# Linear attention and a 3x3 convolution on 32 images: set-up rewritten, value and output weights joined per head, order changed, last image written out

## The reference

```python
# layer 0: linear attention, 4 heads of 32 channels, 4 learned memory positions
xn  = x / norm * g * C ** 0.5                    # norm over channels, of the group-normed x
q, k, v = split(einsum('bchw,oc->bohw', xn, w_qkv))
k, v = concat([mem_k, k]), concat([mem_v, v])    # along the pixels
q = softmax(q, over the head's channels) * dh ** -0.5
k = softmax(k, over pixels)
context = einsum('bhdn,bhen->bhde', k, v)
out = einsum('bhde,bhdn->bhen', context, q)
x = x + einsum('bchw,oc->bohw', out, w_out) + b_out
# layer 1: 3x3 convolution where (j - i) % 4 == 0, 1x1 convolution elsewhere
x = x + conv3x3(gn(x), w3 * m3) + einsum(w1 * ~m3, gn(x)) + b1.sum(axis=1)
```

## Time and profile before

| what | value |
|---|---|
| median of 3 runs | 2020.36 us (2018.03 to 2023.75) |
| the profiled execution, its time | 2011.88 us |
| its span, first to last instruction | 2010.1 us |
| mean granted TensorE clock | 0.983 of full |
| busy: PE, DVE, ACT, POOL | 94%, 83%, 68%, 66% |
| DMA queue of the loads, stores and copies | 73.8% of 16 engines |

### The profile page before, as it was taken

One profiled execution on the slowest core, in us unless ns is written; L12 is line 12 of the kernel. 1 busy time (PEld: TensorE's weight loads), 2 busy tenths in 40 slices (PEclk: granted clock), 3 DMA queues, 4 the chain that ended last, 5 costly groups with the idle time before them and its releaser, 6 DMA issues.

```text
span 2010.1 us, 50737 instructions
## 1 busy us (share of the span) xinstructions
PE 1882.8 (94%) x21199; PEld 1017.6 (51%) x21199; DVE 1676.3 (83%) x3144; ACT 1361.0 (68%) x1476; POOL 1321.8 (66%) x737
## 2 busy tenths in 40 slices
PE   2889999999999999999999999999999999999995
PEld 0445545555544555554555554455554455555452
DVE  5688888888888888888888888888888888888862
ACT  2667668767667776766876766777766777676660
POOL 5566667776667676666776665777666767666652
PEclk9789999999999999999999999999999999999997
DMA  5358778787877797876878777778787778787665
GB/s 108 64 96 176 162 159 162 160 177 160 165 162 160 156 183 154 174 163 159 161 161 170 165 163 156 154 167 177 152 175 154 162 155 180 148 174 162 130 132 129
DMA packets 349427, 312.96 MB, mean 156 GB/s; under 512 B 299152, under 2 KB 299920, under 8 KB 341008
## 3 DMA queue, kind: packets, MB, share of 16 engines
q1 hardware_dynamic: 347712, 308.73, 73.8%
q10 hardware_dynamic: 1168, 0.98, 0.2%
q0 software_dynamic: 320, 0.01, 0.0%
HBM read 68.10 MB, written 67.11 MB: 67 GB/s over the span
## 4 chain that ended last, share of the span: by engine, by line
PE 66%; DVE 17%; SPq 9%; DMA 4%; issue 2%; ACT 1%; POOL 0%; ACTq 0%
PE pair_ps L813 21%; PE pair_ps L795 8%; PE pair_ps L756 6%; PE pair_ps L804 4%; PE bank_ps L710 4%; DVE u L1121 4%; DVE km L1124 3%; PE pair_ps L776 3%; SPq L320 2%; DVE yg_lo L1171 2%; SPq L333 2%; DVE image L1176 2%; DVE bn L1045 2%; PE bank_ps L786 2%; PE pair_ps L741 2%; PE bank_ps L765 2%
## 5 line engine op out<-in xcount | busy, mean ns | idle before, releaser
L813 PE MATMUL pair_ps<-replicas,w_rep 96*32 96x512 f16 x8192 | 490.5, 384 | 11.7 <-DMA replicas<-yg_lo 11.3
L441 POOL TENSOR_TENSOR u_lo<-u,u_hi 128x1024 f16<-128x1024 f32 x128 | 270.3, 2144 | 274.3 <-ACT u_hi L558 274.3
L444 POOL TENSOR_TENSOR exp_kT_lo<-exp_kT,exp_kT_hi 128x1024 f16<-128x1024 f32 x128 | 273.6, 2137 | 206.4 <-ACT exp_kT_hi L567 203.4
L813 PEld LDWEIGHTS pair_ps<-replicas,w_rep 96*32 96x32 f16 x8192 | 204.4, 96 | 260.1 <-issue 85.2
L447 POOL TENSOR_TENSOR u_lo<-exp_q,u_hi 128x1024 f16<-128x1024 f32 x128 | 272.6, 2141 | 45.5 <-ACT u_hi L573 44.7
L558 ACT ACTIVATE u_hi<-u 128x1024 f16<-128x1024 f32 x128 | 134.9, 1054 | 134.8 <-DVE u L1121 130.1
L1176 DVE SCALAR_TENSOR_TENSOR image<-pair_ps,image 128x512 f32<-128x512 f32 x256 | 176.0, 688 | 55.0 <-PE pair_ps L813 49.4
L437 POOL TENSOR_SCALAR u<-image,st 128x1024 f32<-128x1024 f32 x128 | 179.6, 1411 | 40.4 <-DVE st L1075 40.4
L564 ACT ACTIVATE exp_kT<-pair_ps,zcol 128x1024 f32<-128x1024 f32 x128 | 142.0, 1109 | 90.3 <-PE pair_ps L756 87.7
L573 ACT ACTIVATE u_hi<-exp_q 128x1024 f16<-128x1024 f32 x128 | 133.9, 1046 | 97.1 <-DVE exp_q L1163 97.1
L454 POOL TENSOR_TENSOR yg_lo<-u,yg_hi 128x1024 f16<-128x1024 f32 x64 | 152.9, 2390 | 68.5 <-ACT yg_hi L581 68.5
(11 more groups left out here) (179 smaller groups left out, 4601.2 us busy)
## 6 DMA issues: line engine op xcount, KB each, us to landing
image<-in_x SPq DMA_DIRECT2D x256, 256.0 KB, 4.8
out<-image SPq DMA_DIRECT2D x512, 128.0 KB, 2.3
replicas<-yg_hi SPq DMA_DIRECT2D x256, 165.0 KB, 3.6
replicas<-yg_hi SPq DMA_DIRECT2D x256, 107.2 KB, 2.3
replicas<-yg_lo SPq DMA_DIRECT2D x128, 165.0 KB, 4.1
replicas<-yg_lo SPq DMA_DIRECT2D x128, 107.2 KB, 2.3
uT_hi<-u_hi SPq DMA_TRANSPOSE x128, 4.4
uT_lo<-u_lo SPq DMA_TRANSPOSE x128, 4.2
```

The source lines that it names most:

```text
L441: pool.tensor_tensor(px(UL, v), px(U, v), px(UH, v), ALU.subtract).then_inc(ul_ready, 1)
L444: pool.tensor_tensor(KL[:, v % 2], KT[:, v % 2], KH[:, v % 2], ALU.subtract).then_inc(kl_ready, 1)
L813: mm = pe.matmul(conv_ps[32 * r:32 * r + 32, j % 2], w_rep[0:32 * SLOTS, tap, r], rep[:, j * ROWS + dy:(j + 1) * ROWS + dy, dx:dx + SIDE], ...
```

## The change

Four things change together.

**Set-up.** SP waits until image 0 has landed before it issues the loads of image 1. ACT permutes the weights (three copies), DVE no longer does, and so `x_seed` and `x_scale` of image 0 don't stand behind them. PE turns query, key and output weights first and ten convolution blocks after them; the value weights aren't turned. ACT keeps the turned taps in SBUF after the first `norm_power`, rounds them after the last `high_u` of image 0, and DVE splits them behind the first `rows_q`; SP replicates the convolution weights after step 1 instead of step 0. Four large memsets go to DVE (`spread` and `minus_max` were POOL's).

**Per head.** The set-up multiplies value weights and output weights of each head into `value_out` (128 x 4 x 128) and the memory values into `memory_out`. `value_context` and `mask_context` are gone; `mix_weights` has eight float32 products of 128x32 weights on 128 columns, each head on its own column group. Context and memory part are turned undivided, and `split_mix` divides.

**Order.** `square_y` 2 and 3 follow `exp_memory`, `y_moments` follows `max_q` 2, `x_stats` 0 stands before `rows_q` and `low_y` 0 before the other three, `queries` 3 uses another pair, `norm_sums` stand elsewhere, and more, as the diff has it.

**The end.** `over_samples` makes 33 steps instead of 35, and then `drain(c, e)` writes out the end of image 31 (c) and of 30 (e): DVE makes its group norm and low parts alone, the replicating DMAs and stores are shared by SP and ACT, and the statistics of image 31 start before the last chunks of image 30.

SP, before the loop, in `step` and in `drain`:

```diff
-for k in range(PRELOADED):
-    load(k, 0)
-    load(k, 1)
+load(0, 0)
+load(0, 1)
+for h in range(2):
+    sp.wait_ge(x_in[h][0], at_load(0))
+load(1, 0)
+load(1, 1)
...
+        if e is not None:
+            sp.wait_ge(out_ready, at(e, CHUNKS, 6))
+            store(e, 2)
         if a is not None:
             sp.wait_ge(ul_ready, at(a, UNITS, 1))
             turn_u(a, 0)
...
+def drain(c, e):
+    sp.wait_ge(hi_ready, at(c, UNITS, 2))
+    sp.wait_ge(conv_done, at(e, CHUNKS, 4))
+    replicate_high_part(c, 0, range(2))
+    sp.wait_ge(lo_even, at(c, UNITS // 2, 1))
+    sp.wait_ge(lo_odd, at(c, UNITS // 2, 1))
+    replicate_low_part(c, 0, range(2))
...
+    sp.wait_ge(out_ready, at(c, CHUNKS, 8))
+    store_part(c, 3, range(2))
```

ACT, in `norm_power`, `high_u`, `step` and `drain`, and before the loop:

```diff
+        if first(s):
+            act.wait_ge(setup_pe, TAPS_TURNED)
+            act.activation(taps32[:, 0:8], conv_ps.rearrange("p k (t o) -> p (k t) o", o=P), ACT.Copy,
+                           scale=W_SCALE).then_inc(setup_act, 1)
...
+        if first(s) and v == UNITS - 1:
+            act.wait_ge(setup_act, TAPS_KEPT)
+            act.activation(w_hi, taps32[:, 0:TAPS], ACT.Copy).then_inc(setup_act, 1)
...
             exp_memory()
+        if c is not None:
+            act.wait_ge(y_ready, at(c, UNITS, 3))
+            square_y(c, 2)
+            act.wait_ge(y_ready, at(c, UNITS, 4))
+            square_y(c, 3)
+        if a is not None:
             act.wait_ge(kT_done, at(a, UNITS, 1))
...
+            act.wait_ge(q_soft, at(a, UNITS, 3))
+            high_q(a, 2)
         if p is not None:
             act.wait_ge(norm_sum, at(p, UNITS, 2))
             act.wait_ge(xg_ready, at(p, UNITS, 4))
             square(p, 3)
...
+def drain(c, e):
+    act.wait_ge(y_ready, at(c, UNITS, 3))
+    square_y(c, 2)
+    act.wait_ge(y_ready, at(c, UNITS, 4))
+    square_y(c, 3)
+    act.wait_ge(y_stat, at(c, Y_STEPS, Y_STEPS))
+    high_y(c, 0)
+    high_y(c, 1)
...
+    replicate_high_part(c, 0, range(2, RES))
+    high_y(c, 2)
+    act.wait_ge(conv_done, at(e, CHUNKS, 8))
+    high_y(c, 3)
...
+    replicate_low_part(c, 0, range(2, RES))
...
+act.wait_ge(weights_in, 16 * WEIGHT_DMAS)
+act.activation(perm_qkv, raw_qkv.rearrange("p t (i r) -> p t r i", r=RES), ACT.Copy).then_inc(setup_act, 1)
+act.activation(perm_w1, raw_w1.rearrange("p (i r) -> p r i", r=RES), ACT.Copy).then_inc(setup_act, 1)
+act.activation(perm_w3, raw_w3.rearrange("p (i r t) -> p t r i", r=RES, t=TAPS), ACT.Copy).then_inc(setup_act, 1)
```

PE, its functions, `step` and `drain`:

```diff
+def fold_values():
+    pe.wait_ge(setup_dve, HEADS_READY)
+    heads = wo_heads.rearrange("p h o -> p (h o)")
+    pe.matmul(pair_ps[0][:, 0:BANK], perm_qkv[:, 2].rearrange("p r i -> p (r i)"), heads, start=True, stop=True)
+    pe.wait_ge(col_in, 16 * COL_DMAS)
+    pe.matmul(pair_ps[0][0:MEM, BANK:2 * BANK], mv[:], heads, start=True, stop=True).then_inc(setup_pe, 1)
...
     def norm_sums(s, v, ps):
...
+        if first(s) and v == UNITS - 1:
+            fold_values()
...
-    def value_context(ps):
-        pe.matmul(ps[:, 0:P], wqkvT[:, 2], AT_sb[:], start=True, stop=False)
-        pe.matmul(ps[:, 0:P], mvT[0:MEM], pkT_sb[0:MEM], start=False, stop=True).then_inc(mix_pe, 1)
     def mix_weights(ps):
-        pe.matmul(ps[:, 0:P], ctxT_sb[:], woT[:], start=True, stop=True).then_inc(mix_pe, 1)
+        for h in range(HEADS):
+            q = slice(DH * h, DH * h + DH)
+            pe.matmul(ps[q, 0:P], AT_sb[:, q], value_out[:, h], start=True, stop=False)
+        for h in range(HEADS):
+            q = slice(DH * h, DH * h + DH)
+            mm = pe.matmul(ps[q, 0:P], pkT_sb[:, q], memory_out[:, h], start=False, stop=True)
+        mm.then_inc(mix_pe, 1)
...
             pe.wait_ge(k_max, at(a, 8, 7))
             turn_k_max(bank_ps[1])
+            rough_q(a, 0, pair_ps[1])
...
         if c is not None:
             conv_dense(c, 0)
+        if a is not None:
+            pe.wait_ge(den_act, at(a, 2, 1))
+            pe.wait_ge(mix_dve, at(a, 7, 2))
+            turn_context(bank_ps[1])
+        if c is not None:
             conv_dense(c, 1)
...
             conv_ring(c, 0)
             conv_ring(c, 1)
         if a is not None:
             pe.wait_ge(den_dve, at(a, 4, 4))
             den_broadcast(a, 0, pair_ps[1])
         if p is not None:
+            if a is not None:
+                pe.wait_ge(mix_dve, at(a, 7, 5))
             pe.wait_ge(sq_ready, at(p, UNITS, 1))
             norm_sums(p, 0, bank_ps[1])
             pe.wait_ge(sq_ready, at(p, UNITS, 2))
             norm_sums(p, 1, bank_ps[1])
         if a is not None:
+            den_broadcast(a, 1, pair_ps[0])
+        if c is not None:
+            pe.wait_ge(out_ready, at(c, CHUNKS, 1))
+            conv_dense(c, 2)
+        if a is not None:
+            pe.wait_ge(q_soft, at(a, UNITS, 1))
+            den_broadcast(a, 2, pair_ps[1])
+        if c is not None:
+            conv_ring(c, 2)
+        if a is not None:
+            mix_weights(bank_ps[0])
+            pe.wait_ge(q_soft, at(a, UNITS, 3))
             den_broadcast(a, 3, pair_ps[1])
+        if c is not None:
+            pe.wait_ge(out_ready, at(c, CHUNKS, 2))
+            conv_dense(c, 3)
+        if a is not None:
+            pe.wait_ge(mix_dve, at(a, 7, 7))
+            pe.wait_ge(el_ready, at(a, UNITS, 1))
+            mix(a, 0, pair_ps[0])
         if p is not None:
             pe.wait_ge(sq_ready, at(p, UNITS, 3))
             norm_sums(p, 2, bank_ps[1])
             pe.wait_ge(sq_ready, at(p, UNITS, 4))
             norm_sums(p, 3, bank_ps[1])
...
+def drain(c, e):
+    pe.wait_ge(out_ready, at(e, CHUNKS, 5))
+    conv_dense(e, 6)
+    pe.wait_ge(y_stat, at(c, Y_STEPS, 4))
+    group_means(1, bank_ps[1], y_group)
+    conv_ring(e, 5)
+    conv_ring(e, 6)
...
+    conv_ring(e, 7)
+    pe.wait_ge(out_ready, at(e, CHUNKS, 7))
+    pe.wait_ge(lo_even, at(c, UNITS // 2, 1))
+    conv_dense(c, 0)
```

DVE, its functions, `step` and `drain`:

```diff
     def norm_guard(s, ps):
...
+        if first(s):
+            dve.wait_ge(setup_pe, FOLDED)
+            dve.tensor_scalar(value_out[:].rearrange("p h o -> p (h o)"), pair_ps[0][:, 0:BANK], gcol[:], None, ALU.mult)
+            make(dve.tensor_copy(memory_out[0:MEM].rearrange("p h o -> p (h o)"), pair_ps[0][0:MEM, BANK:2 * BANK]))
...
+                dve.tensor_scalar(kneg_bf[:, 32:33], km[:, 5:6], -1.0, None, ALU.mult)
+                did(dve.tensor_scalar(kneg_bf[:, 0:1], km[:, 5:6], -1.0, None, ALU.mult))
...
+                did(dve.tensor_tensor(z[:, 0:1], ps[:, P:P + 1], pk_sum[:], ALU.add), wait=False)
+                did(dve.tensor_copy(A_sb[:], ps[:, 0:P]))
+                did(dve.reciprocal(z[:, 1:2], z[:, 0:1]), wait=False)
...
             max_q(a, 1, pair_ps[0])
+            dve.wait_ge(q_rough, at(a, UNITS, 3))
+            max_q(a, 2, pair_ps[1])
         if c is not None:
             dve.wait_ge(y_squared, at(c, UNITS, 4))
             y_moments(c)
...
             x_stats(p, 0)
+        if a is not None:
+            dve.wait_ge(max_turned, at(a, 2, 2))
+            rows_q(a, bank_ps[1])
+        if c is not None:
+            dve.wait_ge(yg_ready, at(c, UNITS, 1))
+            dve.wait_ge(hi_ready, at(c, UNITS, 1))
+            low_y(c, 0)
+        if p is not None and not first(p):
             x_stats(p, 1)
...
+def drain(c, e):
+    dve.wait_ge(y_squared, at(c, UNITS, 4))
+    y_moments(c)
...
+    finish(e, 5)
+    group_norm_y(c, 0)
...
+    last_low_y(c, 2)
+    dve.wait_ge(conv_done, at(e, CHUNKS, 7))
+    finish(e, 6)
+    dve.wait_ge(conv_done, at(e, CHUNKS, 8))
+    finish(e, 7)
```

More of the change, by code:

```diff
@@ L676, in step @@
                     square_y(a, 1)
-                    act.wait_ge(y_ready, at(a, UNITS, 3))
-                    square_y(a, 2)
-                if p is not None:
-                    act.wait_ge(u_ready, at(p, UNITS, 1))
-                    high_u(p, 0)
-            act.wait_ge(setup_pe, 1)
-            for t in range(0, TAPS, 4):
-                n = min(4, TAPS - t)
-                last = act.activation(w_hi[:, t:t + n], tap_ps(t, n).rearrange("p (t o) -> p t o", t=n), ACT.Copy,
-                                      scale=W_SCALE)
@@ L772, in queries @@
             def queries(s, v, ps):
+                if first(s) and v == 0:
+                    pe.wait_ge(const_made, POOL_STEPS)
                 for j in (2 * v, 2 * v + 1):
@@ L1311, in _ @@
+            for t in (kneg_bf, quad_mask, red_norm, red_head):
                 last = dve.memset(t[:], 0.0)
```

439 lines of the change are left out of this document (257 added, 182 removed).

## The result

The changed kernel takes 1961.03 us (median of 4 executions, 1959.35 to 1965.83) where the kernel before took 2022.05 us on the same chip: ratio 0.9704, 95% interval 0.9688 to 0.9721. The forecast was 1962 us, in the range of 1942 to 1987 us. On a second chip the same pair gave 1963.47 and 2013.96 us, ratio 0.9752 (0.9727 to 0.9777). The profiled execution took 1962.26 us, its span is 1960.5 us; the span before was 2010.1 us, so 49.6 us have to be found in the trace.

The account below looks back on a forecast made before the run. PE was taken to bound the steady state, 85% of the span. Gains of 37 us in the steps, 10 at the start and 11 at the end make 58: 2020.4 - 58 = 1962 us, range 1942 to 1987.

Parts of the forecast that it names:

- Small products: PE's eight new value and output weight products take 0.65 us instead of 1.15: gain 0.5 us a step.
- Norm sums: PE's second pair of `norm_sums` no longer waits for ACT's last square: gain 0.6 us a step, bounds 0 and 0.6.
- PE's 1.1 us arrive as about 0.8: Behind a step's first ring products, PE's 1.1 us gain shrinks to about 0.8 because DVE's residual and norm chain limits it.
- Context wait: PE's wait for the context's DVE steps shrinks from 0.34 to 0.1 us a step.
- Group mean of layer 1: `y_moments` behind `max_q` 2 makes PE wait a new 0.3 us before this mean, in front of keys 2.
- Statistics: PE's wait for the next image's statistics mostly goes with DVE's new order: 0.55 of 0.60 us a step gained.
- Ring 0's wait: At a step's first ring products, more steps wait for `low_y` replicas issued by SP: 0.1 us a step lost.
- Sum a step: Steady state: 1.2 us a step gained, 58.4 instead of 59.64, times 31 is 37 us; bounds 0.4 to 1.7.
- Start: First norm broadcast at 37.5 us instead of 47.64: gain 10 us, bounds 6 and 12.
- End: Last image: shorter waits for low parts and replicas, last store and low-clock time: gain 11 us, bounds 7 and 14.
- first rival: Steady gain only a third, through poorly overlapping column groups, late squares or DVE's chain: 1987 us, chance 16%.
- third rival: More gain than forecast, since unprofiled runs have more long steps that go too: 1949 to 1954 us, chance 9%.

Follow-up runs that it names:

- second of before: The kernel before, unchanged, executed and profiled once more: ratio 1.0007 to before, span 2016.4 us against 2010.1 in its first trace.
- image 1 at once: The changed kernel with SP loading image 1 right behind image 0, without waiting for image 0 to land: ratio 0.9768 to the kernel before.

## Why the prediction was right

The total was right, 61 us (50 on the second chip) for 58. That it came within 1 us of the forecast is in part luck: between the two profiles there are 49.6 us, the steps brought less than forecast and the ends more, and the replicas' wait, 12 us in 31 steps more than forecast, was made up for by the long steps that the first profile had too few of (11.4 us between the medians and the profiles). The sum a step also left out what the prediction itself had found ahead of ring 0, 0.3 and 0.15 us of new waits against 0.25 us gained; the 0.2 us did not come. The parts, step by step:

- **Small products**: 0.55 us for 0.65, gain 0.60 for 0.5, the upper bound. The argument that column groups run beside each other holds.
- **Norm sums**: both pairs together take 1.99 us instead of 2.77 (1.10 and 1.67), gain 0.78 for 0.6. As a mechanism right; but its price with the place taken away, 1.8 us in the shortest step, was underestimated by far, because I stopped at ACT's square and did not follow the residuals behind it.
- **"PE's 1.1 us arrive as about 0.8"**: the reason was wrong. Behind ring 0 the shortest step lost 0.56 us (24.18 to 23.62), and no new wait for DVE is there. The rest went into the broadcasts of the denominators: before, two of them stood together, four products in 0.32 us (a row at 1039.31 below); now each stands alone, two products in the same 0.32 us (1253.89 to 1254.21, 1255.21 to 1255.53, 1258.92 to 1259.24). That costs 0.64 us a step, and the prediction did not price it. 0.60 + 0.78 - 0.64 is 0.74; the 0.18 left is in products of the mix and dense products that are parted now.
  On PE's timeline of the kernel before, two broadcasts and the dense product behind them:

```profile
1039.31 0.40 PE L717 MATMUL pair_ps<-parts,spread 32*128 32x512 bf16 x4
1039.63 0.62 PE L804 MATMUL pair_ps<-yg_hi,w_mid 128*128 128x512 f16 x2
```

- **Context wait** 0.34 to 0.1: it is gone. **Group mean of layer 1**, 0.3 us of new wait: it did not come. **Turned key maxima** +0.15: 0.23. Together the shortest step is 0.19 us shorter ahead of ring 0.
- **Statistics**: the wait is gone, as forecast, 0.54 us a step in this trace and 0.74 in the second of before. That DVE's new order removes it is shown for the kernel before. In the new order of the other engines it isn't `low_y` 0's place: back in the old one only 0.2 us a step of the wait return.
- **Ring 0's wait**: the term that was mis-sized. I named SP's list and took 0.1 us a step for it; the wait grew by 0.49 us a step. The sentence before it, that nothing ahead of ring 0 can be gained beyond the short step since SP's list is the same, was nearly right (0.19 us came there), and should have been a price: most of what the statistics gave there, the replicas took.
- **Sum a step**: 0.75 us from the shortest step, 0.54 from the statistics, 0.49 lost at ring 0: 0.8 in the trace against the forecast's 1.2 (bounds 0.4 to 1.7). Against the second trace of before it is 1.04.
- **Start**: 36.53 for 37.5, 11.1 us for 10. That the weights land sooner was priced at 2 us at most (39.5 if they did not); it was 7.8. The 13 us from the weights to the broadcast were too few: it takes 17.4 us (19.15 to 36.53), and 18.1 with image 1 at once. Of the 3.3 us of the first three steps 2.5 are their share of the steps' gain.
- **End**: 12.2 us for 11; the wait behind `finish` 6 is 4.97 for 5.4; that for the replicas, 1.3 us as forecast, is at ring 3 and not at ring 0.

So between these two traces the steps gave less than forecast (25 of 37: 31 steps of 0.82) and the ends more (24 of 21). That is halfway to the first rival, whose reasons (products that do not overlap, late squares) did not occur. The other 11.4 us of the 61 between the medians come from the executions that were profiled: before's lay 10.2 us below its median and this one 1.2 above. The third rival had this part right: the second trace of before has the additional long steps. Of the rule of the Trainium skill ("SBUF — State Buffer", Who interferes with whom) the runs show one thing more: with `low_y` 0 in its new place no image has the 3.9 us form, in either kernel's order, though GpSimd is at work beside it. Both engines still lose time there, 0.6 and 0.9 us in the rows above.

## What to carry to other kernels

- When a wait on the path goes, look up which chain was next, and by how little. Here a queue that only issues DMAs was within 0.6 us of the path in the short steps; that margin, and not the length of the wait, limits the gain. It can be read before the change: the distance from the end of the issue to the start of the waiting instruction is nearly the same in most steps that wait (1.8 us in seven of eight before, 1.7 us in most after).
- Splitting the issue between two queues was worth more here than moving it: four copies moved gave nothing, two moved gave 16 us.
- In an order fitted by hand the terms do not add: the same swap was worth 0.6 us by the rows of one order and 1.8 us in the other. And count what a move parts as well as what it joins.

## What the hardware showed

- Four bfloat16 products with 32-row weights on 512 columns, each on its own row group, take 0.32 us together (1039.31 to 1039.63 before); put apart by other work, each two take 0.32 us as well (1253.89 to 1254.21 after).
- The issue of a transposing DMA of the same size holds SP for 1.3 us in the median of the 256 in the trace after, and for 2.9 to 4.8 us at one place of every step (`u_lo` of the third unit).
- 2 MB of another load beside them made the weights land 7.05 us later (19.15 to 26.20 us), while image 0 was not later (18.92 and 19.06 us).
- A low part on VectorE and a normalisation pass on GpSimd that meet lengthen each other: 1.85 us instead of 1.22, and 4.51 us for three passes instead of 3 times 1.20.
